# Moving the C multiplies of the scan between VectorE and GpSimd in whole states

## The reference, cut to what matters

```python
dA = jnp.exp(delta_t[:, :, None] * A[None, :, :])
dBu = delta_t[:, :, None] * B_t[:, None, :] * u_t[:, :, None]
h = dA * h + dBu
y = jnp.einsum('bds,bs->bd', h, C_t)
```

## Time and profile before

| | us |
|---|---|
| median of 3 runs | 1238.01 (1236.98 to 1244.79) |
| the profiled execution | 1237.58 |
| its span, first to last instruction | 1235.8 |
| VectorE busy over the span | 942.1 (76%) |
| GpSimd busy | 818.5 (66%) |
| TensorE matmuls busy | 968.2 (78%) |
| ScalarE busy | 720.7 (58%) |

### The profile page before, as it was taken

The page is one execution under the profiler, slowest core; times in us unless marked ns, Lnnn a source line. Parts: engine busy times, 40 slices in busy tenths (PEclk is TensorE's granted clock), DMA queues, the critical chain, the costliest instruction groups (busy, mean ns, idle before and its releaser), DMA issues. The chain is left out here.

```text
span 1235.8 us, 15659 instructions
## 1 busy us (share of the span) xinstructions
PE 968.2 (78%) x4332; PEld 486.8 (39%) x4347; DVE 942.1 (76%) x1625; ACT 720.7 (58%) x1406; POOL 818.5 (66%) x747
## 2 busy tenths in 40 slices
PE   5689797979797877466665548898898988489996
PEld 2233343424233322343443424454444543235553
DVE  3799999999999999566565226787677784359996
ACT  3777686868676653323333313776666667278772
POOL 1898989899999997244442354575847643467773
PEclk9899999989899989768787655999989999789998
DMA  5552534424251510600000023332323220000001
GB/s 175 229 240 91 195 128 169 172 103 173 102 207 68 228 47 1 108 15 1 0 0 0 1 80 88 91 105 63 95 64 92 79 79 2 0 1 10 18 9 34
DMA packets 34878, 103.84 MB, mean 84 GB/s; under 512 B 3627, under 2 KB 22443, under 8 KB 23979
## 3 DMA queue, kind: packets, MB, share of 16 engines
q1 hardware_dynamic: 34807, 103.03, 24.2%
HBM read 93.71 MB, written 8.91 MB: 83 GB/s over the span
## 5 line engine op out<-in xcount | busy, mean ns | idle before, releaser
L554 PE MATMUL m_yac<-m_hC,ident 128*128 128x512 f32 x512 | 266.5, 641 | 73.6 <-DVE m_hC L315 46.5
L506 POOL TENSOR_TENSOR m_dBu<-m_du,m_Bt 128x1024 f32<-128x1024 f32 x128 | 299.3, 2356 | 6.5 <-DVE m_dA L306 5.1
L1109 DVE TENSOR_REDUCE a_nm<-a_s 128x2 f32<-128x512 f32 x256 | 170.4, 686 | 95.3 <-PE a_s L1348 89.4
L306 DVE TENSOR_TENSOR_SCAN m_dA<-m_dA,m_dBu 128x512 f32<-128x512 f32 x184 | 221.7, 1219 | 15.1 <-ACT m_dA L444 12.1
L1296 ACT ACTIVATE a_pT<-a_s 128x512 f32<-128x512 f32 x256 | 150.9, 600 | 96.9 <-PE a_s L1348 95.9
L554 PEld LDWEIGHTS m_yac<-m_hC,ident 128*128 128x128 f32 x512 | 93.1, 198 | 225.5 <-issue 105.1
L444 ACT ACTIVATE m_dA<-m_delta,mprm 128x510 f32<-128x510 f32 x256 | 169.4, 675 | 0.3
L1348 PE MATMUL a_s<-ks,qs 72*128 72x256 bf16 x512 | 106.5, 294 | 33.0 <-DMA ks<-parts 22.7
L315 DVE TENSOR_TENSOR m_hC<-m_dA,m_Ct 128x512 f32<-128x512 f32 x184 | 123.3, 670 | 0.0
L516 POOL TENSOR_TENSOR m_hC<-m_hS,m_Ct 128x512 f32<-128x512 f32 x72 | 94.6, 1314 | 31.7 <-DVE m_hS L306 31.5
L1644 POOL TENSOR_TENSOR b_h_rest<-b_h_full,b_h_parts 128x512 f32<-128x512 f32 x64 | 77.2, 1212 | 44.9 <-ACT b_h_parts L1669 36.8
(11 more groups left out here) (218 smaller groups left out, 1816.5 us busy)
## 6 DMA issues: line engine op xcount, KB each, us to landing
m_Bt<-bcd SPq DMA_DIRECT2D x32, 1024.0 KB, 5.6
m_Ct<-bcd SPq DMA_DIRECT2D x32, 1024.0 KB, 6.6
qs<-parts SPq DMA_DIRECT2D x16, 576.0 KB
ks<-parts SPq DMA_DIRECT2D x48, 192.0 KB
parts<-a_part SPq DMA_DIRECT2D x32, 192.0 KB, 2.2
out<-x_all SPq DMA_DIRECT2D x8, 256.0 KB, 2.3
mprm<-in_mprm SPq DMA_DIRECT2D x1, 1203.0 KB, 6.6
vx<-in_vrow SPq DMA_DIRECT2D x4, 256.0 KB
```

The source lines that it names most:

```text
L306: nc.vector.tensor_tensor_scan(out, decay, dBu[:, g % RD], 0.0, ALU.mult, ALU.add).then_inc(scan_ready, 1)
L506: nc.gpsimd.tensor_tensor(dBu[:, g % RD:g % RD + CH], du[:, n % 2], Bt[:, s].unsqueeze(1).broadcast_to([P, CH, GTOK]), ALU.mult).then_inc( ...
L554: return nc.tensor.matmul(out, lhsT, rhs, start=start, stop=stop)
L1109: nc.vector.tensor_reduce(nm[:, slot % 2, q, 2 * pair:2 * pair + 2], s1[i % 2][:], AX.X, ALU.max, negate=True).then_inc(max_ready, 1)
```

## The change

`POOL_C` marks both halves of the states 0, 4, 7, 10 and 13. GpSimd multiplies a whole state with one instruction of 128 x 1024, with C repeated over the two halves, and VectorE keeps both units of the other eleven states. GpSimd's multiply waits for the second half's scan and for room for both in hC, and releases both at once. VectorE's first multiply in each quarter of C waits for that quarter's load.

```diff
--- before.py
+++ after.py
@@ -170,7 +170,7 @@
     RA, RD, RH, RS = 4, 8, 8, 4
     LAG = 4
     NQ, QS = 4, NS // 4
-    POOL_C = [c == 1 and s * 9 % 16 < 9 for s in range(NS) for c in range(CH)]
+    POOL_C = [s * 5 % 16 < 5 for s in range(NS) for c in range(CH)]
     SKIP_AT = 14
     ctx = ExitStack()
     with ctx:
@@ -309,7 +309,7 @@
                 s = i // CH
                 g = UNITS * n + i
                 dve.wait_ge(scan_ready, g + 1)
-                if s % QS == 0:
+                if on_dve(0, i) == on_dve(0, 2 * QS * (s // QS)):
                     dve.wait_ge(c_in[s // QS], 16 * (n + 1))
                 wait(dve, acc_done, g - RH + 1)
                 nc.vector.tensor_tensor(hC[:, g % RH], dA[g % RA][:].rearrange("p a b -> p (a b)"), Ct[:, s],
@@ -507,14 +507,16 @@
                                         Bt[:, s].unsqueeze(1).broadcast_to([P, CH, GTOK]),
                                         ALU.mult).then_inc(drive_ready, CH)
 
-            def times_c(n, i):
-                s = i // CH
-                g = UNITS * n + i
-                pool.wait_ge(scan_ready, g + 1)
+            def times_c(n, s):
+
+                g = UNITS * n + CH * s
+                at = on_pool(n, CH * s) % RS
+                pool.wait_ge(scan_ready, g + CH)
                 pool.wait_ge(c_in[s // QS], 16 * (n + 1))
-                wait(pool, acc_done, g - RH + 1)
-                nc.gpsimd.tensor_tensor(hC[:, g % RH], hS[:, on_pool(n, i) % RS], Ct[:, s],
-                                        ALU.mult).then_inc(hcp_ready, 1)
+                wait(pool, acc_done, g + CH - RH)
+                nc.gpsimd.tensor_tensor(hC[:, g % RH:g % RH + CH], hS[:, at:at + CH],
+                                        Ct[:, s].unsqueeze(1).broadcast_to([P, CH, GTOK]),
+                                        ALU.mult).then_inc(hcp_ready, CH)
 
             def shifts(m):
                 pool.wait_ge(stat_chain, 2 * m + 2)
@@ -539,8 +541,8 @@
                     if n < GROUPS and i % CH == 0:
                         drive(n, i // CH)
                     a, b = (n, i - LAG) if i >= LAG else (n - 1, UNITS + i - LAG)
-                    if 0 <= a < GROUPS and POOL_C[b]:
-                        times_c(a, b)
+                    if 0 <= a < GROUPS and POOL_C[b] and b % CH == 0:
+                        times_c(a, b // CH)
                     if i in (26, 27) and n + 1 < GROUPS:
                         sum_delta(n + 1, i - 26)
                     if n == GROUPS and i == 28:
```

## The result

The changed kernel takes 1249.92 us in the median of six runs (1244.38 to 1253.99) where the kernel before, on the same chip, takes 1237.86: a ratio of 1.0097 [1.0057, 1.0136]. The forecast was 1242 with a range of 1231 to 1249; the time lies 0.9 us above it.

A forecast was written before the change was run, and what follows sets the result against it. VectorE's queue was taken to set the scan's length. Group 0 +4, groups 1 to 6 +2, group 7 -1.2 and tail -0.8 sum to +4 on 1237.6 us: 1242, with an 8-in-10 range of 1231 to 1249.

The forecast's parts named there:

- TensorE's feedback: At group turns: du first makes TensorE about 1.0 late, so drive 15 wins next; groups alternate between -0.6 and +1.3.
- rival 2: At group ends, GpSimd's drive 15 starts before VectorE's du in every group: six times +1.3, total 1245 to 1250; chance 0.18.
- The price of the whole-state multiply: On GpSimd, a 128 x 1024 multiply by C costs 2.3 us, like a drive; five per group add no load.
- rival 3: On GpSimd, the whole-state multiply takes 3.44 us, so its queue exceeds VectorE's: total 1250 to 1256; chance 0.06.
- VectorE's 22 multiplies: In each group VectorE makes 22 multiplies instead of 23: 8 x 0.59 = 4.7 us less.
- The convolution's wait: VectorE's wait at scan 11, behind the convolution's SiLUs on ScalarE, grows from 1.0 to 1.6 us per group.
- the gate: VectorE's wait at scan 7, behind the gate's SiLU on ScalarE, falls from 0.8 to 0.2 us per group.
- du's lock: At group ends VectorE's two du and GpSimd exclude each other: the pair costs 2.55 with du first, 4.5 with drive 15 first.
- the residual: VectorE's residual waits 0.5 us for a late TensorE in the group after one that ended with du first.
- Group 0: TensorE starts 3.8 us later behind GpSimd's first whole multiply, delaying scan 11: +4, between 0 and +6.
- Last group: Group 7, without du, changes by -1.2 (multiply and gate); the tail's shorter wait for TensorE gives -0.8.
- a forecast margin of 0.2 us: At group ends GpSimd's drive 15 and VectorE's first du start within 0.2 us of each other.

The follow-up runs named there:

- the halves: GpSimd keeps the changed kernel's five states, each multiplied in two 128 x 512 instructions instead of one; 1235.57 us, 0.9973 of the kernel before.
- state 13 in halves: The changed kernel with state 13 alone multiplied in two instructions of 128 x 512, the other four states whole; 1242.91 us, 1.0018 of the kernel before.
- first execution: First profiled execution of the changed kernel, nothing edited; span 1242.6 us, scan 467.40.
- second execution: Second profiled execution of the changed kernel, nothing edited; span 1249.2 us, scan 476.29.
- three edits together: The changed kernel, whole states, with state 1 instead of 0, both du behind unit 27 and x turned earlier; 1256.77 us, 1.0132 of the kernel before.

## Why the prediction missed

**The step that failed** is the one on TensorE's feedback: "the two outcomes should alternate: a group of the first kind changes by -0.6 (the multiply), one of the second by +1.3". An execution keeps one course through all six groups. Where drive 15 is first, six groups give +12.3, rival 2's mechanism, which I had at six times 1.3 and 0.18; four of these groups are 1.6 to 1.7 longer than before, and the two with the slow convolution 2.8 and 2.9. Where du is first, they give +4.1 and not -3.6, because the groups pay at the turn instead: the multiply of state 13, 2.3 us and held 0.45 by du, leaves TensorE idle for 5.69 and it starts again at the lower clock. Before, half of that state came from GpSimd, and TensorE waited 1.59 for it:

```profile
145.69 1.12 PE L554 MATMUL m_yac<-m_hC,ident 128*128 128x512 f32 x2 [1.59 <-POOL m_hC L516]
```

I had priced the long instruction of state 13 for VectorE's queue, and for TensorE only that of state 0; the waits of yg and scan 0 at the turn stood in the sum at nothing. That its length is the cause of these waits is shown by the halves, where they are gone and the group is 56.63, and by state 13 in halves, where they are gone but for one.

That the time lies only 0.9 above the range is in part luck. The scan lost 9 to 19 us where the sum had 4, and the unedited rest gave back 4.4 to 4.7 that the sum didn't have.

**Right.** The price of the whole-state multiply, start distance 2.30 as for a drive; rival 3 is out. GpSimd in group 0, first execution:

```profile
46.02 2.35 POOL L517 TENSOR_TENSOR m_hC<-m_hS,m_Ct 128x1024 f32<-128x1024 f32 x1
48.32 4.67 POOL L506 TENSOR_TENSOR m_dBu<-m_du,m_Bt 128x1024 f32<-128x1024 f32 x2
```

VectorE's 22 multiplies, 0.53 per group. The convolution's wait in full groups, 1.52 against a forecast of 1.6, and none listed at the gate against 0.2. du's lock: pairs of 2.06 and 1.69 recorded, start distances 1.98 and 1.61, 3.6 together, where I had 4.5. The place of the feedback, the residual: 0.89 against 0.5.

**Sizes.** Group 0: +4.95, +4.1 and +4.65 against +4. Slower full groups: in group 2 of the second execution, -0.6 (multiply), +1.3 recorded in du (3.7 against 2.4), +0.6 at the residual (0.89 against 0.3) make 58.5 of the 58.70 measured. Last group: the forecast was -1.2 and -0.8; it gains nothing (+0.3) or loses 1.8. As it is cut here VectorE makes 22 multiplies in it before and after, so only the gate's 0.6 is gained; its last yg now waits 2.84 for TensorE where it waited 2.1, and in the slower course the residual waits 1.67 and yg 2.67:

```profile
503.95 1.29 DVE L327 TENSOR_TENSOR m_yg<-m_yac,m_gate 128x512 f32<-128x512 f32 x2 [2.84 <-PE m_yac L556]
```

**Left open.** The rest of the kernel is 4.4 to 4.7 us shorter after the change in all three executions, without an edit there. Over the other kernels it goes from 734 to 745, and with it the totals stray from the scans by some 5 us. The traces show the place: it is gained in the attention. 384 us behind the last yg the changed kernel is still 1.3 to 1.8 later there than the kernel before, 535 us behind it 4.0 to 4.5 earlier. I did not find the cause. Nor is it settled what chooses the course of an execution. Group 0 ends with du held in all three; the course goes with the clock of TensorE at the start of group 1, but the idle stretches ahead of it are much alike (2.39, 2.81 and 2.54), and what set the level there is not shown. That each course keeps itself up is read from the traces; no run forces one kernel from one into the other with all else equal.

## What to carry to other kernels

Joining two instructions into one that costs the same (2.30 against 2 x 1.2) is not free where another engine consumes the halves in order: it gets the first half a whole instruction late, and an engine with two clock levels may then restart at the lower one. Ask of a longer instruction not only what its own queue pays but who waits for its first half. Where two engines lock each other, the order of their starts decides; a forecast margin of 0.2 us between them (0.7 and 0.8 were measured, one each way) may fall the same way in every group, so price the kernel at both sides rather than at their mean. It may be better to remove the meeting: one du instruction in place of two, one unit earlier, gave the kernel before 0.5%.

## What the runs showed of the hardware beside this

- Two VectorE instructions in a row with both inputs in SBUF do not keep GpSimd out: its 2.3 us instruction starts between them, and the pair takes 4.8 us instead of 1.3.
- Very short GpSimd operations are held as well. With one du at 145.28 the power (rstd), 1.02 otherwise, takes 2.02:

```profile
145.42 2.02 POOL L532 TENSOR_TENSOR m_rstd<-m_veps,neg_half 128x4 f32<-128x4 f32 x1
```

- TensorE's restart at the lower clock costs about 1 us for two accumulations (2.07 against 1.12) and up to 2 for the eight matmuls behind (5.04 to 5.62 against 3.60). The length of one idle stretch doesn't tell whether it comes: behind 2.64 the two accumulations took 2.04 in one group of the kernel before and 1.10 in another, and with three edits together they took 1.10 behind 3.84 and only the convolution was slow:

```profile
164.67 1.10 PE L557 MATMUL m_yac<-m_hC,ident 128*128 128x512 f32 x2 [3.84 <-DVE m_yg L327]
165.60 5.29 PE L557 MATMUL m_pp<-m_xT,m_wk 128*128 128x512 f32 x8
```
